# A whitening, window attention and mixture-of-experts kernel: the inverse root of its variances as one power operation on GpSimd

## The chip, the cores and the metric

The kernel runs on one core of one Trainium2 chip. The metric is the device time of one execution in microseconds, as the median of several executions.

## The reference

The input x is (16, 56, 56, 64) in float32, that is 50,176 tokens of 64 channels. Three stages follow one another.

```python
# 1. whitening (_iter_norm_whiten): groups of 16 channels, statistics over all tokens
cov = (1 - EPS) * cov + EPS * eye;  sigma = cov / trace
for _ in range(5): P = (3 * P - P @ P @ P @ sigma) / 2
x = gamma * (P / sqrt(trace)) @ (x - mu) + beta
# 2. attention in a window of 33 tokens, per image (3136 tokens)
kv = _ln_t(t)                                  # (v - mean) / sqrt(var + 1e-5), over 64 channels
out = softmax(scores * 64 ** -0.5) @ windows
out = (out - mean(out)) * rsqrt(var(out) + 1e-5) * gamma + beta
t = t + out
# 3. mixture of experts: 8 experts, top 2
n = _ln_t(t)
t = t + moe(n)    # n + sum over the two experts of weight * (gelu(n @ w1 + b1) @ w2 + b2)
```

So there are three layer norms per token: of the whitened tokens, of the attention's output and of the sum that goes into the experts.

## The kernel before, in words

All engines have instruction streams written out by hand, and semaphores alone order them against each other. There are three parts.

The first part (to about 78 us) loads x once, builds the Gram matrix on TensorE and column sums on VectorE, and computes the whitening matrix in a chain of small operations. GpSimd prepares constants in that time.

The middle part (about 78 to 535 us) does the whitening, the attention and the routing. The 16 images go in pairs (H = 2); a chunk is NB = 7 blocks of 64 tokens of both images of a pair (CH = 448 columns on 128 partitions), CPI = 7 chunks make a pair, and there are G = 56 chunks. The work is a software pipeline: in step g each engine does stage d of chunk g - d, so that a step holds one stage each of seven chunks. In the step function of each engine, `has(d)` says whether stage d has a chunk. The stages: 0 transposes and whitens a chunk, squares it for its variance and makes its norm xn; 1 transposes xn into keys; 2 computes the scores and their exponential; 3 does the product with the values, and scales the attention's output to t_s; 4 takes bn_stats of the residual sum and makes its norm tn; 5 transposes tn and spills it to HBM; 6 computes the router's logits. The routing (top 2 of 8) of finished pairs is cut into single VectorE operations, one per step (`route`).

The order inside a step, with the lines of the profile:

- TensorE: transposes of the x tiles of chunk g (L971, L964 out of `to_paired`), router logits of chunk g - 6 (L981, L984), whitening of chunk g (L979, L981, L984), product with the values of g - 3 (L1060), transposes of xn of g - 1 (L971, L964) and of tn of g - 5 (L971, L964), scores of g - 2 (L1082, L1087). L979 waits for L521's copy.
- ScalarE: copy of the transposed x (L521), copy of the logits (L526), square of the whitened chunk (L534) and its copy (L537), square of the attention's sums (L542), copy of the keys (L548), copy of the transposed tn (L558) and its store, exponential of the scores (L569), and last the logarithm (L574) and the exponential with scale -0.5 (L576) of the variances of the step, 7 per norm and up to 21 columns. L574 waits for the variances (semaphore s_w), L576 for L574.
- VectorE: sums of the squares (L790), the variances of stages 0 and 3 (L793, L795), bn_stats of stage 4, seven times (L800), and the variance out of them (L803 to L809), which raises s_w; one routing operation; then it waits for L576 and does a Newton step in three operations (L818, L820, L822) that corrects the approximate root; xn (L828), stored by the DMA queues as rows, from which the values come back with windows; seven scalings of the attention's output (L834); the scaled mean (L842), tn (L843) and a correction column (L845), which signals tn.
- GpSimd: beta added to the whitened chunk (L479, after xn), and the residual sum t_s + yb (L487), which waits for t_s of its chunk and for L845 of the step, and which bn_stats of the next step reads.
- SyncE issues the loads of x, the row stores after xn, and the loads of the values.

`sm` is the small tile for all of this: slot 4 has the variances (times C = 64), slots 6 and 7 the logarithm and the approximate root, 8 and 9 the Newton step and the result. `norms(has)` gives the range of the three norms that exist in the step.

The last part (about 535 us to the end) runs the experts, four pairs of them for each chunk, and is not touched.

Of the kernel before, what the change touches and what calls it, by code (L numbers as in the profile page):

```python
# [29 lines left out]
NB = 7  # L30
# [3 lines left out]
C = 64  # L34
# [9 lines left out]
EPS_LN = 1e-5  # L44
# [9 lines left out]
def hybrid_kernel(nc, x, g0, b0, g1, b1v, rw, w1, b1, w2, b2, k_eye, k_fold, k_group, k_block, k_band,  # L54
                  k_rank, k_sel, out):
    f32, bf16, f32r = mybir.dt.float32, mybir.dt.bfloat16, mybir.dt.float32r
    ALU, ACT, AX = mybir.AluOpType, mybir.ActivationFunctionType, mybir.AxisListType
# [8 lines left out]
    SCALE = float(C) ** -0.5  # L66
# [12 lines left out]
    with ctx:  # L79
        def sb(name, shape, dt=f32):  # L80
            return ctx.enter_context(nc.sbuf_tensor(name, shape, dt))
# [4 lines left out]
        def sem(name):  # L86
            return ctx.enter_context(nc.semaphore(name))
# [100 lines left out]
        sq = sb("sq", [128, 2, NB, C + 1])  # L188
# [5 lines left out]


        sm = sb("sm", [128, 10, 3, NB])
        top = sb("top", [128, 5, NB * CPI])

        tn_rows = t_s[:, 0:2, :, :].rearrange("p k b c -> p k (b c)")
# [15 lines left out]
        s_cd, s_cp, s_ca = sem("chain_dve"), sem("chain_pe"), sem("chain_act")  # L215
        s_x2 = [sem(f"x2_in{i}") for i in range(7)]
        s_xt, s_xts, s_y, s_ys, s_yb = sem("xt"), sem("xt_copied"), sem("y"), sem("y_copied"), sem("yb")
        s_v, s_w, s_ln, s_r, s_n = sem("norm_steps"), sem("norm_var"), sem("norm_log"), sem("norm_rsqrt"), sem("norm_newton")
        s_red, s_xn = sem("pv_squares_summed"), sem("xn")
        s_xnt, s_kts = sem("xn_t"), sem("keys_copied")  # L220
        s_pad, s_xw, s_vd = sem("pads_zeroed"), sem("xn_rows_stored"), [sem(f"values_in{i}") for i in range(2)]
# [1 line left out]
        s_sqy, s_sq, s_t = sem("y_squared"), sem("pv_squared"), sem("t_scaled")  # L223
# [13 lines left out]
        def wait(eng, s, n):  # L237

            if not isinstance(n, int) or n > 0:
                eng.wait_ge(s, n)  # L240
# [36 lines left out]
        def norms(has):  # L277

            lo = 0 if has(0) else 1 if has(3) else 2
            hi = 3 if has(4) else 2 if has(3) else 1  # L280
            return lo, hi
# [126 lines left out]
        def _(pool):  # L408
            v = nc.gpsimd
# [11 lines left out]
            v.memset(ones_h[:, :], 1.0)  # L421
            v.memset(white[:, :, :], 0.0)
            v.memset(ones, 1.0)
            v.memset(v_a[:, :, :, C], 1.0)
            zeros = sq[0:WIN].rearrange("p k b c -> p (k b c)")[:, 0:NP // 2 * H * C]
            v.memset(zeros, 0.0).then_inc(s_zero, 1)
# [45 lines left out]
            v.memset(keys_t[:, WIN + CPI * CH:], 0.0).then_inc(s_zero, 1)  # L472

            def step(g, c, has):
                if has(1):
                    q, cq = g - 1, prv(c, 1)
                    wait(pool, s_xn, g + 1 if has(0) else G)
                    ybc = yb[:, cq, :, 0:C]
                    v.tensor_tensor(ybc, ybc, bet1[:, :].unsqueeze(1).to_broadcast([128, NB, C]), ALU.add).then_inc(s_yb, 1)  # L479
                if has(3):  # L480
                    q, cq = g - 3, prv(c, 3)
                    sl = SLOT2[cq]
                    wait(pool, s_t, q + 1)
                    wait(pool, s_yb, q + 1)
                    if has(4):
                        wait(pool, s_tn, q)
                    v.tensor_tensor(resid[:, bass.ds(q * CH, CH)].rearrange("p (b c) -> p b c", b=NB), t_s[:, sl],  # L487
                                    yb[:, cq, :, 0:C], ALU.add).then_inc(s_t2, 1)
# [13 lines left out]
        def _(act):  # L502
            a = nc.scalar
# [13 lines left out]
            def step(g, c, has):  # L517
# [10 lines left out]
                if has(0):  # L528
                    wait(act, s_y, g + 1)
                    wait(act, s_w, g)  # L530
                    y_s = p01[:, 1, 0:NB * (C + 1)].rearrange("p (b c) -> p b c", b=NB)
                    if g == 0:
                        act.wait_ge(s_pad, 16 * 4)
                    a.activation(sq[:, 0], y_s, ACT.Square).then_inc(s_sqy, 1)  # L534
                    wait(act, s_t2, g - 6)
                    wait(act, s_tn, g - 6)
                    a.activation(yb[:, c], y_s, ACT.Copy).then_inc(s_ys, 1)  # L537
                if has(3):
                    q = g - 3
                    wait(act, s_o, q + 1)  # L540
                    wait(act, s_w, g)
                    a.activation(sq[:, 1], sums(q).rearrange("p (b c) -> p b c", b=NB),  # L542
                                 ACT.Square).then_inc(s_sq, 1)
                if has(1):
                    q, cq = g - 1, prv(c, 1)
                    wait(act, s_xnt, q + 1)
# [18 lines left out]
                if has(2):  # L565
# [1 line left out]
                    wait(act, s_s, q + 1)  # L567

                    a.activation(prob[:, :, :], p34[0:KEYS, :, 0:CH], ACT.Exp, scale=SCALE).then_inc(s_p, 1)  # L569
                lo, hi = norms(has)  # L570
                if lo < hi:

                    wait(act, s_w, g + 1)
                    a.activation(sm[:, 6, lo:hi, :], sm[:, 4, lo:hi, :], ACT.Ln, scale=1.0 / C).then_inc(s_ln, 1)  # L574
                    wait(act, s_ln, g + 1)
                    a.activation(sm[:, 7, lo:hi, :], sm[:, 6, lo:hi, :], ACT.Exp, scale=-0.5).then_inc(s_r, 1)  # L576

            for g in range(G):
                step(g, g % 7, lambda d, g=g: d <= g)
# [63 lines left out]
        def _(dve):  # L643
            v = nc.vector
# [16 lines left out]
            for k in range(2):  # L661
                last = v.tensor_reduce(colsum2[:, k, :], colsum.rearrange("p n c -> p c n"), AX.X, ALU.add)
# [116 lines left out]
            def step(g, c, has):  # L779
                lo, hi = norms(has)  # L780
# [9 lines left out]
                    v.tensor_reduce(sm[:, 0, of, :], sq[:, of, :, 0:C], AX.X, ALU.add).then_inc(s_red, 1)  # L790
                    wait(dve, s_red, g + 1)
                if has(0):
                    last = v.tensor_scalar(sm[:, 4, 0, :], sm[:, 0, 0, :], C * EPS_LN, None, ALU.add)  # L793
                if has(3):
                    last = v.scalar_tensor_tensor(sm[:, 4, 1, :], sq[:, 1, :, C], C * EPS_LN, sm[:, 0, 1, :], ALU.mult, ALU.add)  # L795
                if has(4):
                    wait(dve, s_t2, g - 3)
                    t4 = resid[:, bass.ds((g - 4) * CH, CH)].rearrange("p (b c) -> p b c", b=NB)
                    for b in range(NB):
                        last = v.bn_stats(st[:, b, :], t4[:, b, :])  # L800
                    last.then_inc(s_v, 1)
                    wait(dve, s_v, (g - 4) * 3 + 1)
                    v.tensor_tensor(sm[:, 0, 2, :], st[:, :, 1], st[:, :, 4], ALU.add)  # L803
                    v.tensor_tensor(sm[:, 1, 2, :], st[:, :, 1], st[:, :, 4], ALU.subtract)
                    v.scalar_tensor_tensor(sm[:, 2, 2, :], st[:, :, 2], C * EPS_LN, st[:, :, 5], ALU.add, ALU.add).then_inc(s_v, 1)
                    wait(dve, s_v, (g - 4) * 3 + 2)
                    v.tensor_tensor(sm[:, 4, 2, :], sm[:, 1, 2, :], sm[:, 1, 2, :], ALU.mult).then_inc(s_v, 1)
                    wait(dve, s_v, (g - 4) * 3 + 3)
                    last = v.scalar_tensor_tensor(sm[:, 4, 2, :], sm[:, 4, 2, :], C / 4.0, sm[:, 2, 2, :], ALU.mult, ALU.add)  # L809
                if lo < hi:  # L810
                    last.then_inc(s_w, 1)
                im, k = route_at(g, 0)
# [2 lines left out]
                if lo < hi:  # L815

                    wait(dve, s_r, g + 1)
                    v.tensor_tensor(sm[:, 8, lo:hi, :], sm[:, 4, lo:hi, :], sm[:, 7, lo:hi, :], ALU.mult).then_inc(s_n, 1)  # L818
                    wait(dve, s_n, g * 3 + 1)
                    v.scalar_tensor_tensor(sm[:, 8, lo:hi, :], sm[:, 8, lo:hi, :], -0.5 / C, sm[:, 7, lo:hi, :], ALU.mult, ALU.mult).then_inc(s_n, 1)  # L820
                    wait(dve, s_n, g * 3 + 2)
                    v.scalar_tensor_tensor(sm[:, 9, lo:hi, :], sm[:, 8, lo:hi, :], 1.5, sm[:, 7, lo:hi, :], ALU.add, ALU.mult).then_inc(s_n, 1)  # L822
                    wait(dve, s_n, g * 3 + 3)
                if has(0):
                    wait(dve, s_xnt, g)
                    wait(dve, s_xw, 48 * g)
# [404 lines left out]
```

## Time and profile before

| | us |
|---|---|
| median of 3 executions | 1111.7 |
| lowest and highest | 1108.69, 1125.13 |
| the profiled execution's own time | 1112.64 |
| its span in the profile | 1110.9 |
| TensorE busy | 1048.4 |
| VectorE busy | 904.3 |
| ScalarE busy | 565.4 |
| GpSimd busy | 148.3 |

The profile has one execution. PE is TensorE (PEld its weight loads), DVE is VectorE, ACT is ScalarE, POOL is GpSimd; L12 is line 12 of the kernel. A row of the timeline reads: start in us, duration in us, engine, line, operation, output<-input, shapes, count, and in brackets how long the engine stood idle before it and what ended that. In groups by line, the columns are busy us and mean ns of one, then the idle time before them. PEclk is TensorE's granted clock in tenths of full speed, in 40 equal slices; 1.00 in a table of windows is 2.4 GHz and 0.50 is 1.2 GHz. The chain that ended last is followed back from the last instruction through what released each one.

### The profile page before, as it was taken

Reading aid. Unit: us, or ns where it says so; the run is one execution under the profiler, and the core shown is the slowest. Engines: PE = TensorE matmul, PEld = TensorE weight load, DVE = VectorE, ACT = ScalarE, POOL = GpSimd, SP = SyncE. Lnnn points to the kernel's source line nnn. Section 1 sums busy time; section 2 is a strip of 40 time slices with the busy share of each in tenths; the row PEclk is TensorE's granted clock in tenths of the full one; section 3 lists DMA queues with packets and bytes.
Section 4 is the critical chain, followed back from the end, with each engine's and each line's share of the span. In section 5 each row is a group of like instructions: output and inputs, shape, how many; then the busy total and the mean of one; then the engine's idle time right before and its main releaser. Section 6 shows DMA issues by size and latency. Waiting matters only on the chain.

```text
span 1110.9 us, 26094 instructions
## 1 busy us (share of the span) xinstructions
PE 1048.4 (94%) x9158; PEld 692.8 (62%) x9158; DVE 904.3 (81%) x2575; ACT 565.4 (51%) x917; POOL 148.3 (13%) x179
## 2 busy tenths in 40 slices
PE   7947999999999999998799999999999999999998
PEld 7935777777777777776455555555555555555553
DVE  6944888887888887887788888888888888888785
ACT  0014655655566555653455555555555555555553
POOL 7021232232223222231000000000000000000000
PEclk9959999998999999995799999999999999999999
DMA  9604555554555555543122222222222222222221
GB/s 290 238 9 105 142 131 147 136 133 113 143 138 136 142 135 137 136 120 90 42 67 70 71 66 67 71 70 66 74 66 67 68 73 66 70 71 66 67 71 44
DMA packets 244750, 111.51 MB, mean 100 GB/s; under 512 B 199392, under 2 KB 242656, under 8 KB 243888
## 3 DMA queue, kind: packets, MB, share of 16 engines
q1 hardware_dynamic: 235456, 96.91, 35.1%
q10 hardware_dynamic: 8064, 12.85, 3.4%
q8 instruction: 51, 0.84, 0.3%
q0 software_dynamic: 1136, 0.56, 0.2%
q14 instruction: 43, 0.35, 0.1%
HBM read 71.60 MB, written 38.67 MB: 99 GB/s over the span
## 4 chain that ended last, share of the span: by engine, by line
PE 82%; ACT 9%; DVE 4%; issue 3%; DMA 2%; SPq 0%; POOL 0%; DVEq 0%; ACTq 0%; POOLq 0%
PE p L1138 17%; PE p L1113 16%; PE p L1123 10%; PE p L1087 7%; PE p L971 7%; ACT prob L569 5%; PE p L1060 4%; PE p L964 4%; PE p L981 4%; ACT xt_s L521 3%; PE p L1082 3%; DMA resid<-in_x_dram 2%; PE p L1134 2%; PE p L979 2%; PE p L1008 2%
## 5 line engine op out<-in xcount | busy, mean ns | idle before, releaser
L586 ACT ACTIVATE arena<-p,b_s 128x896 f32<-128x896 f32 x224 | 225.5, 1007 | 231.0 <-PE p L1113 229.6
L890 DVE TENSOR_TENSOR arena<-arena,p 128x896 f32<-128x896 f32 x224 | 242.5, 1083 | 76.4 <-PE p L1123 74.8
L1138 PE MATMUL p<-arena,w_s 128*64 128x448 f32 x896 | 215.2, 559 | 0.3 <-DVE arena L890 0.3
L1113 PE MATMUL p<-thl,w_hi 128*128 128x448 f32 x448 | 165.2, 450 | 0.4 <-DVE thl L862 0.4
L1113 PE MATMUL p<-thl,w_lo 128*128 128x448 f32 x448 | 127.3, 365 | 0.0
L1123 PE MATMUL p<-arena,selector 128*128 128x448 bf16 x448 | 123.9, 358 | 1.8 <-DVE arena L890 1.4
L1123 PEld LDWEIGHTS p<-arena,selector 128*128 128x128 bf16 x448 | 25.4, 97 | 159.0 <-issue 116.9
L1113 PEld LDWEIGHTS p<-thl,w_hi 128*128 128x128 f32 x448 | 85.6, 192 | 21.2 <-issue 0.6
L479 POOL TENSOR_TENSOR yb<-yb,bet 128x448 f32<-128x448 f32 x56 | 59.2, 1058 | 253.5 <-DVE xn_s L828 253.5
L569 ACT ACTIVATE prob<-p 96x896 f32<-96x896 f32 x56 | 51.1, 912 | 78.2 <-PE p L1087 78.2
L1113 PEld LDWEIGHTS p<-thl,w_lo 128*128 128x128 f32 x448 | 84.9, 189 | 7.6
L1087 PEld LDWEIGHTS p<-arena 64*96 64x96 f32 x1568 | 74.2, 167 | 20.3 <-issue 20.3
L790 DVE TENSOR_REDUCE sm<-sq 128x14 f32<-128x896 f32 (+1 forms) x59 | 61.2, 1038 | 29.4 <-ACT sq L542 22.6
L1087 PE MATMUL p<-arena 64*96 64x64 f32 x1568 | 82.0, 255 | 0.0
L834 DVE SCALAR_TENSOR_TENSOR t_s<-p,sm,gam 128x64 f32<-128x64 f32 x392 | 80.0, 276 | 0.1
L1138 PEld LDWEIGHTS p<-arena,w_s 128*64 128x64 f32 x896 | 49.5, 135 | 44.0 <-issue 34.0
L534 ACT ACTIVATE sq<-p 128x455 f32<-128x455 f32 x56 | 30.8, 550 | 89.6 <-PE p L984 89.6
L487 POOL TENSOR_TENSOR resid<-t_s,yb 128x448 f32 (+1 forms) x56 | 59.2, 1057 | 81.3 <-DVE comb L845 80.9
L862 DVE TENSOR_TENSOR thl<-arena,thl 64x896 fp32r<-64x896 f32 x56 | 60.7, 1085 | 2.6 <-ACT thl L599 0.9
L971 PE MATMUL p<-eye,arena 128*128 128x128 f32 x336 | 59.4, 286 | 0.7 <-DVE arena L927 0.7
L800 DVE BATCH_NORM_STATS2 st<-resid 128x6 f32<-128x64 f32 x392 | 54.8, 211 | 1.3 <-POOL resid L487 1.3
L599 ACT ACTIVATE thl<-arena 64x896 fp32r<-64x896 f32 x56 | 53.0, 946 | 4.7 <-DMA arena<-tn_spill 3.2
(177 smaller groups left out, 1640.6 us busy)
## 6 DMA issues: line engine op xcount, KB each, us to landing
tn_spill<-tnt_s ACTq DMA_DIRECT2D x56, 224.0 KB, 2.7
arena<-tn_spill SPq DMA_DIRECT2D x56, 224.0 KB, 3.4
t_s<-tn_spill SPq DMA_DIRECT2D x56, 224.0 KB, 2.5
arena<-in_x_dram SPq DMA_DIRECT2D x112, 96.0 KB, 2.6
xn_rows<-xn_s SPq DMA_DIRECT2D x56, 192.0 KB, 2.1
out_dram<-arena SPq DMA_DIRECT2D x112, 96.0 KB, 1.8
resid<-in_x_dram SPq DMA_DIRECT2D x6, 1568.0 KB, 14.2
v_a<-xn_rows SPq DMA_DIRECT2D x56, 168.0 KB, 3.3
```

Of the source, the lines that this page charges most:

```text
L479: v.tensor_tensor(ybc, ybc, bet1[:, :].unsqueeze(1).to_broadcast([128, NB, C]), ALU.add).then_inc(s_yb, 1)
L569: a.activation(prob[:, :, :], p34[0:KEYS, :, 0:CH], ACT.Exp, scale=SCALE).then_inc(s_p, 1)
L586: a.activation(hid[:, j % 2, :].rearrange("p (h n) -> p h n", h=H), (p34 if j % 2 == 0 else p56)[:, :, 0:CH], ACT.Gelu, bias=b1_s[:, j:j + ...
L790: v.tensor_reduce(sm[:, 0, of, :], sq[:, of, :, 0:C], AX.X, ALU.add).then_inc(s_red, 1)
L834: last = v.scalar_tensor_tensor(t_s[:, sl3, b, :], o_s[:, b, 0:C], sm[:, 9, 1, b:b + 1], gam1[:, :], ALU.mult, ALU.mult)
L862: v.tensor_tensor(thl[64:128, c], tn_in[:, c].rearrange("p (h n) -> p h n", h=H), thl[0:64, c].bitcast(f32), ALU.subtract).then_inc(s_lo, 1)
L890: v.tensor_tensor(gated[:, j % 2, :].rearrange("p (h n) -> p h n", h=H), hid[:, j % 2, :].rearrange("p (h n) -> p h n", h=H), p01[:, :, 0: ...
L971: t.transpose(dst[:, b * 128:(b + 1) * 128], src[:, b * 128:(b + 1) * 128], eye[:, :])
L1087: last = t.matmul(p34[0:KEYS, h, b * BLK:(b + 1) * BLK], keys_t[r, at_b:at_b + KEYS], keys_t[r, at_b + WIN:at_b + WIN + BLK], start=False, ...
L1113: last = t.matmul(bank[:, h, 0:CH], w[:, 128 * j:128 * (j + 1)], thl[:, c, h, :], start=(k == 0), stop=(k == 1))
L1123: last = t.matmul(p01[:, h, 0:CH], selector[:, (4 * h + j) * 128:(4 * h + j + 1) * 128], ct_s[:, c, :], start=True, stop=True)
L1138: last = t.matmul(p2[64 * h:64 * h + 64, 0:CH], w2_s[:, j, :], gated[:, j % 2, h * CH:(h + 1) * CH], start=False, stop=(j == 3))
```

## The change

The variances are now divided by C before the root: Square on ScalarE gets the scale 1/8 (SCALE, whose square is 1/64), and the constants of L793, L807 and L809 follow. GpSimd raises the variances to the power -0.5, with a tile of -0.5 as the second operand, at the head of its step, and gives s_r; the logarithm, the exponential and the three operations of the Newton step are gone. The first part keeps its own logarithm and exponential.

```diff
+        halves = sb("halves", [128, 3, NB])
...
+            v.memset(halves[:, :, :], -0.5)
...
             def step(g, c, has):
+                lo, hi = norms(has)
+                if lo < hi:
+                    wait(pool, s_w, g + 1)
+                    v.tensor_tensor(sm[:, 9, lo:hi, :], sm[:, 4, lo:hi, :], halves[:, lo:hi, :], ALU.pow).then_inc(s_r, 1)
                 if has(1):
...
-                    a.activation(sq[:, 0], y_s, ACT.Square).then_inc(s_sqy, 1)
+                    a.activation(sq[:, 0], y_s, ACT.Square, scale=SCALE).then_inc(s_sqy, 1)
...
-                                 ACT.Square).then_inc(s_sq, 1)
+                                 ACT.Square, scale=SCALE).then_inc(s_sq, 1)
...
-                lo, hi = norms(has)
-                if lo < hi:
-                    wait(act, s_w, g + 1)
-                    a.activation(sm[:, 6, lo:hi, :], sm[:, 4, lo:hi, :], ACT.Ln, scale=1.0 / C).then_inc(s_ln, 1)
-                    wait(act, s_ln, g + 1)
-                    a.activation(sm[:, 7, lo:hi, :], sm[:, 6, lo:hi, :], ACT.Exp, scale=-0.5).then_inc(s_r, 1)
...
-                    last = v.tensor_scalar(sm[:, 4, 0, :], sm[:, 0, 0, :], C * EPS_LN, None, ALU.add)
+                    last = v.tensor_scalar(sm[:, 4, 0, :], sm[:, 0, 0, :], EPS_LN, None, ALU.add)
...
-                    v.tensor_tensor(sm[:, 4, 2, :], sm[:, 1, 2, :], sm[:, 1, 2, :], ALU.mult).then_inc(s_v, 1)
+                    v.scalar_tensor_tensor(sm[:, 4, 2, :], sm[:, 1, 2, :], 0.25, sm[:, 1, 2, :], ALU.mult, ALU.mult).then_inc(s_v, 1)
...
-                    last = v.scalar_tensor_tensor(sm[:, 4, 2, :], sm[:, 4, 2, :], C / 4.0, sm[:, 2, 2, :], ALU.mult, ALU.add)
+                    last = v.scalar_tensor_tensor(sm[:, 4, 2, :], sm[:, 2, 2, :], 1.0 / C, sm[:, 4, 2, :], ALU.mult, ALU.add)
...
                     wait(dve, s_r, g + 1)
-                    v.tensor_tensor(sm[:, 8, lo:hi, :], sm[:, 4, lo:hi, :], sm[:, 7, lo:hi, :], ALU.mult).then_inc(s_n, 1)
-                    wait(dve, s_n, g * 3 + 1)
-                    v.scalar_tensor_tensor(sm[:, 8, lo:hi, :], sm[:, 8, lo:hi, :], -0.5 / C, sm[:, 7, lo:hi, :], ALU.mult, ALU.mult).then_inc(s_n, 1)
-                    wait(dve, s_n, g * 3 + 2)
-                    v.scalar_tensor_tensor(sm[:, 9, lo:hi, :], sm[:, 8, lo:hi, :], 1.5, sm[:, 7, lo:hi, :], ALU.add, ALU.mult).then_inc(s_n, 1)
-                    wait(dve, s_n, g * 3 + 3)
```

## Rows read from the trace of the kernel before

**Rows 1.** The page: busy time of each engine, TensorE's clock in 40 slices, the chain that ended last
```profile
PE 1048.4 (94%) x9158; PEld 692.8 (62%) x9158; DVE 904.3 (81%) x2575; ACT 565.4 (51%) x917; POOL 148.3 (13%) x179
...
PEclk9959999998999999995799999999999999999999
...
PE 82%; ACT 9%; DVE 4%; issue 3%; DMA 2%; SPq 0%; POOL 0%; DVEq 0%; ACTq 0%; POOLq 0%
```

**Rows 2.** Timeline of 212.5 to 222.5 us, rows of ScalarE and TensorE (columns as below)
```profile
213.05 0.91 ACT L569 ACTIVATE prob<-p 96x896 f32<-96x896 f32 x1 [1.30 <-PE p L1087]
...
213.86 0.21 ACT L574 ACTIVATE sm<-sm 128x21 f32<-128x21 f32 x1
214.10 0.22 ACT L576 ACTIVATE sm<-sm 128x21 f32<-128x21 f32 x1
214.22 0.62 ACT L521 ACTIVATE xt_s<-p,neg_mean 128x448 f32<-128x448 f32 x1
...
214.44 0.29 PE L984 MATMUL p<-router,tnt_s 128*64 128x8 f32 x4
...
214.99 0.35 PE L979 MATMUL p<-bet_rows,ones_h 128*128 128x455 bf16 x1 [0.25 <-ACT xt_s L521]
...
222.41 0.35 PE L979 MATMUL p<-bet_rows,ones_h 128*128 128x455 bf16 x1 [0.25 <-ACT xt_s L521]
```

**Rows 3.** Who waited for whom in 100 to 500 us (total us, times, longest us)
```profile
PE p L979 <- ACT xt_s L521: 14.9, 51, 1.2
```

**Rows 4.** The same timeline, rows of VectorE and GpSimd, and the transposes of tn
```profile
215.00 0.63 DVE L828 TENSOR_TENSOR xn_s<-yb,sm 128x448 f32<-128x448 f32 x1
...
215.71 1.04 POOL L479 TENSOR_TENSOR yb<-yb,bet 128x448 f32<-128x448 f32 x1 [4.15 <-DVE xn_s L828]
...
217.50 0.17 DVE L845 TENSOR_TENSOR comb<-yb,sm 128x7 f32<-128x7 f32 x1
...
217.76 0.55 PE L971 MATMUL p<-eye,tn_s 128*128 128x128 f32 x3
217.85 1.09 DVE L790 TENSOR_REDUCE sm<-sq 128x14 f32<-128x896 f32 x1 [0.19 <-ACT sq L542]
...
217.94 1.06 POOL L487 TENSOR_TENSOR resid<-t_s,yb 128x448 f32 x1 [1.19 <-DVE comb L845]
...
219.13 0.98 DVE L800 BATCH_NORM_STATS2 st<-resid 128x6 f32<-128x64 f32 x7
...
220.71 0.17 DVE L809 SCALAR_TENSOR_TENSOR sm<-sm 128x7 f32<-128x7 f32 x1
220.79 0.56 DVE L752 SCALAR_TENSOR_TENSOR arena<-arena 128x392 f32<-128x392 f32 x1
...
222.42 0.63 DVE L828 TENSOR_TENSOR xn_s<-yb,sm 128x448 f32<-128x448 f32 x1
```

**Rows 5.** Groups by line, shapes apart, of the whole span
```profile
L754 DVE TENSOR_TENSOR top<-top 128x49 f32<-128x49 f32 x8 | 1.6, 203 | 0.0
...
L454 POOL TENSOR_TENSOR arena<-arena 128x193 f32<-128x193 f32 x2 | 1.1, 543 | 0.2
...
L759 DVE RECIPROCAL top<-top 128x49 f32<-128x49 f32 x2 | 0.9, 456 | 0.0
```

**Rows 6.** Timeline of 505 to 530 us, the drain of the middle part
```profile
513.83 0.90 PE L971 MATMUL p<-eye,tn_s 128*128 128x128 f32 x3 [0.92 <-DVE comb L845]
...
523.11 0.90 PE L971 MATMUL p<-eye,tn_s 128*128 128x128 f32 x3 [1.30 <-DVE comb L845]
```

**Rows 7.** Timeline of 245 to 258 us, a step in which the clock fell
```profile
245.08 0.35 PE L979 MATMUL p<-bet_rows,ones_h 128*128 128x455 bf16 x1 [0.25 <-ACT xt_s L521]
...
247.07 1.78 PE L1060 MATMUL p<-v_a,prob 96*64 96x65 f32 x28 [0.70 <-issue]
...
257.58 0.56 PE L979 MATMUL p<-bet_rows,ones_h 128*128 128x455 bf16 x1
```

**Rows 8.** Busy time of 100 to 110 us (PE, PEld, DVE, ACT, POOL, then granted clock)
```profile
100.00:110.00 10.00, 6.88 (x98) 5.35 (x95) 6.51 (x30) 5.49 (x12) 2.09 (x2) 1.00 0.57 123
```

More of the change, by code:

```diff
@@ L217, in hybrid_kernel @@
         s_xt, s_xts, s_y, s_ys, s_yb = sem("xt"), sem("xt_copied"), sem("y"), sem("y_copied"), sem("yb")
-        s_v, s_w, s_ln, s_r, s_n = sem("norm_steps"), sem("norm_var"), sem("norm_log"), sem("norm_rsqrt"), sem("norm_newton")
+        s_v, s_w, s_r = sem("norm_steps"), sem("norm_var"), sem("norm_rsqrt")
         s_red, s_xn = sem("pv_squares_summed"), sem("xn")
```

## The prediction

> **What bounds the kernel now.** I began with the page: TensorE is busy 94% of the span, holds 82% of the chain that ended last, and its clock is at full speed in most slices [rows 1]. The change touches only the middle part (about 78 to 535 us, 56 steps of one chunk each), so I went to the timeline of one undisturbed step. From one L979 to the next it lasts 222.41 - 214.99 = 7.42 us [rows 2]. Read downwards, those rows show a closed ring: the scores end, ScalarE takes the exponential (L569), then L574 and L576, which the change removes, and only then the copy L521, on which TensorE's L979 waits. TensorE had finished the router products at 214.44 + 0.29 = 214.73 and stood idle for 0.25 us. The table of waits says that this is the rule: 51 such waits with 14.9 us in 100 to 500 us, of which only the first ones are long (up to 1.2 us) [rows 3]. So a step is TensorE's own work, 7.42 - 0.25 = 7.17 us, and 0.25 us of waiting for ScalarE.
>
> Beside it runs a second ring, over VectorE and GpSimd, nearly as long [rows 4]. Start with L828 (xn) at 215.00. The last VectorE instruction of the step, L845, ends at 217.67, 2.67 us later. The residual sum on GpSimd (L487) starts 0.27 us later, takes 1.06 us and ends at 219.00; bn_stats (L800) of the next step reads its result, I allow 0.10 us between them (at most 0.13 is to be seen), and from the start of L800 to the end of L809, which gives the variances free, go 220.88 - 219.13 = 1.75 us. From there to the next L828 at 222.42 it is 1.54 us. The sum is 2.67 + 0.27 + 1.06 + 0.10 + 1.75 + 1.54 = 7.39 us: this ring has 0.03 us of slack against 7.42. Whoever speeds up the first ring meets the second at once.
>
> **The change part by part.** Call P the time from the end of L809 to the start of L828. Before, P = 1.54 us: ScalarE is held by L569, does two small activations, and then VectorE does three steps (L818, L820, L822). All five go. In their place P = delay to GpSimd + power + delay back. From the end of L828 (215.63) to L479 on GpSimd (215.71) I read 0.08 us [rows 4]; back I allow 0.10 us. GpSimd is idle then: L487 has ended at 219.00, the variances come at 220.88, and the next L479 waits for xn. The routing operation, which stands between L809 and the wait on VectorE, still runs beside it (L752 here, 0.56 us [rows 4], hidden by any longer P).
>
> *ScalarE's side.* L521 would follow L569 as L574 does now: 213.86 instead of 214.22, 0.36 us earlier. L979 follows 0.77 us after the start of L521, so at 214.63, while TensorE is free at 214.73. The step loses the whole 0.25 us and becomes TensorE's 7.17 us. In the 49 steps with the short wait that is 49 x 0.25 = 12.3 us. In five early ones, where TensorE waits longer, 5 x 0.36 = 1.8 us.
>
> *What the second ring allows.* The step is max(7.17, 5.85 + P), with 5.85 = 7.39 - 1.54. The full gain needs P up to 1.32 us; P = 1.57 gives the old 7.42; 2% more (22 us over 50 steps, 0.44 each, so 7.86) needs P = 2.01. The other consumer, the transposes of tn (L971), starts at 217.76, 0.09 us after L845 ends [rows 4]; its slack becomes 0.09 + (1.54 - P) - 0.25, used up at P = 1.38, so it asks for the same.
>
> *The power itself* is in no row. Lower end: as an addition. On GpSimd 193 elements take 0.543 us [rows 5] and 448 take 1.06 [rows 4], so 2.03 ns an element and 0.15 us fixed; 21 elements would take 0.19 us. For a harder function the nearest row is VectorE's reciprocal: 456 ns for 49 elements against 203 ns for a two-input operation of that size [rows 5]. That is 5.2 ns more on top of about 1.07 ns an element ((630 - 203) / (448 - 49), from L828), 5.8 times as much. If a power is a logarithm, a product and an exponential in software, and each counts as a reciprocal on GpSimd, it is 3 x 5.8 x 2.03 x 21 = 0.74 us, and 0.89 us with the fixed part. I take this value. For the upper end I take ten such functions instead of three, 2.63 us; nothing in the rows excludes it, or more. With 0.89, P = 0.08 + 0.89 + 0.10 = 1.07 us, under 1.32.
>
> In terms of the power alone the three marks are therefore 1.14 us (full gain), 1.39 us (no gain) and 1.83 us (2% slower).
>
> *The drain.* After the last chunks the transposes of tn wait for VectorE (0.92 and 1.30 us, [rows 6]), because ScalarE's L574 stands behind an exponential that waits for TensorE. The power does not stand there; these 2.2 us go, and I count 2.0.
>
> *Costed at nothing.* The memset of the constants is one small instruction at the start, under the loads. The scale in Square and the constants in L793, L807 and L809 change no instruction count. L542's output feeds L790 as before.
>
> *Sum* against the profiled execution's own 1112.64 us: 1112.64 - 12.3 - 1.8 - 2.0 = 1096.5. That execution is 0.9 us above the median of the three (1111.7), so 1095.6 by the median; I say 1096.
>
> A rule that speaks against it: on GpSimd, L479 and L487 take 1.04 and 1.06 us [rows 4], beside VectorE work that has one operand in PSUM or is a one-input reduction, so no row shows a GpSimd operation beside a two-input SBUF operation. The Trainium skill (GPSIMD Engine Reference, section "Key points") says that GpSimd shares its SBUF interfaces with VectorE and contends with instructions that have two SBUF inputs; several routing operations are just that.
>
> **The rivals.**
> 1. *The power is slow and the second ring takes over* (the other side of zero). Place: VectorE waits ahead of L828; behind it are queued xn, the seven scalings of the attention output, tn, and on GpSimd L479 and L487, which wait for them. It decides from a power of 1.39 us. With 2.0 us P = 2.18, the step 8.03 us, 50 x 0.61 = 30 us more: 1142; with the upper end of 2.63 us 50 x 1.24 = 62 more, 1174. For it: the ring has only 0.03 us of slack now, and the power's price is a guess. Against it: 21 elements are few.
> 2. *Part of the gain.* A power between 1.14 and 1.39 us gives 1096 to 1112; 1105 for the middle.
> 3. *Contention.* The power stands still while the routing operation reads SBUF: 0.56 us more, P = 1.63, step 7.48, 50 x 0.06 = 3 us above the old steps, with the drain about 1114.
> 4. *The clock falls with the new wait.* One step had TensorE waiting 0.70 us before L1060, and its products then ran slow: that step lasted 257.58 - 245.08 = 12.50 us, 5.08 more [rows 7]. If a slow power causes such a wait (from about P = 2) in every other step, 25 x 5.08 = 127 us more, about 1240. Against it: from 100 to 110 us TensorE is busy 6.88 of 10 us with the granted clock at 1.00 [rows 8].
> 5. *More than the sum.* The wait in rows 7 stands ahead of the product with the values, and I take it for their transfer. If xn comes 0.47 us sooner (1.54 - 1.07) the values do too, and that stretch is gone: 5.08 less, 1091; faster by over 2% needs 1089.
> 6. *The removed work is not on the path*: then it stays at 1112. The 0.25 us behind L521 in nearly every step speaks against that, so I fold it into rival 2.
>
> **How the numbers follow.** Forecast (about 1090 to 1101) 0.48; rival 2 0.10; rival 3 0.04; rival 5 beyond 2% 0.05; rival 1 with a loss under 2% 0.09, over 2% 0.20; rival 4 0.04. So faster by over 2% 0.05, within 2% 0.48 + 0.10 + 0.04 + 0.09 = 0.71, slower by over 2% 0.20 + 0.04 = 0.24; 2% is about what a measurement of this kernel tells from no change. The range starts at 1088 (0.03 below it) and goes to 1150 (a power of about 2.1 us; some 0.16 above it). The likeliest case's own range is 1090 to 1101.
>
> **What would show it.** In the profile after: no wait of L979 for L521, steps of 7.17 us, L521 0.36 us sooner after L569, a power row on GpSimd near 0.9 us, L828 about 1.07 us after L809, TensorE busier than 94%. Wrong is the estimate if the power's row is above 1.14 us; wrong is the arithmetic of the second ring if the step is not 5.85 + P then, or if VectorE still waits ahead of L828 for something other than the power. If L979 still waits with L521 early, another producer was hidden behind it.

## The result: 17% slower, and the profile after

The changed kernel takes 1308.74 us in the median of four runs (1306.98 to 1311.81), the kernel before 1112.42 us beside it; the ratio is 1.173 with a 95% interval of 1.166 to 1.180. The forecast was 1096 us in a range of 1088 to 1150. Here and below, some executions of a kernel fall into a slower state and are left out of its ratio. The profiled execution took 1306.98 us, with a span of 1305.2 us.

The page of the changed kernel, the same three lines as in [rows 1]:

```profile
PE 1216.1 (93%) x9158; PEld 824.6 (63%) x9158; DVE 873.1 (67%) x2395; ACT 554.3 (42%) x797; POOL 363.7 (28%) x240
...
PEclk9957666666666666666666699999999999999999
...
PE 79%; DVE 10%; POOL 6%; issue 2%; DMA 2%; ACT 1%; SPq 0%; POOLq 0%; DVEq 0%; ACTq 0%
```

TensorE is busy for 1216 us instead of 1048, with the same 9158 matmuls: it has no more to do, but its clock stands at 0.6 in the whole middle part, which now fills 19 slices. GpSimd has come into the chain that ended last with 6%, and VectorE's share has gone from 4% to 10%.

The groups by line and shape show why. The power's line (columns: busy us and mean ns of one, idle time before it):

```profile
L480 POOL TENSOR_TENSOR sm<-sm,halves 128x21 f32<-128x21 f32 x52 | 198.1, 3810 | 184.2 <-DVE sm L808 184.2
...
L480 POOL TENSOR_TENSOR sm<-sm,halves 128x14 f32<-128x14 f32 x4 | 10.9, 2725 | 13.8 <-DVE sm L794 8.2 <-DVE sm L808 5.6
...
L480 POOL TENSOR_TENSOR sm<-sm,halves 128x7 f32<-128x7 f32 x4 | 6.2, 1561 | 9.3 <-DVE sm L792 8.6 <-DVE sm L808 0.7
```

A power on 21 elements takes 3.81 us in the mean, on 14 elements 2.73 and on 7 elements 1.56. Each of these means mixes two durations (3.70 and 3.96 us for 21 elements), of which the longer comes from contention with VectorE, taken up below. The shorter ones are 3.70, 2.60 and 1.49 us; that is (3.70 - 1.49) / 14 = 158 ns an element and about 0.39 us fixed. An addition costs 2.03 ns an element [rows 4, 5]; the power costs 78 times that. The prediction had 0.89 us, and 2.63 us as the upper end.

A step in the timeline of the changed kernel, rows that answer to [rows 2] and [rows 4] (L575 is the exponential of the scores that was L569; L527 the copy L521; L972 was L979; L808 was L809; L821 was L828; L964 was L971; L838, L493 and L799 were L845, L487 and L800):

```profile
247.59 0.91 ACT L575 ACTIVATE prob<-p 96x896 f32<-96x896 f32 x1 [1.30 <-PE p L1080]
247.77 0.17 DVE L808 SCALAR_TENSOR_TENSOR sm<-sm 128x7 f32<-128x7 f32 x1
247.85 0.56 DVE L745 TENSOR_TENSOR arena<-arena,rank 128x392 f32<-128x392 f32 x1
...
248.02 3.96 POOL L480 TENSOR_TENSOR sm<-sm,halves 128x21 f32<-128x21 f32 x1 [4.50 <-DVE sm L808]
...
248.40 0.62 ACT L527 ACTIVATE xt_s<-p,neg_mean 128x448 f32<-128x448 f32 x1
...
248.99 0.29 PE L977 MATMUL p<-router,tnt_s 128*64 128x8 f32 x4
...
249.21 0.37 PE L972 MATMUL p<-bet_rows,ones_h 128*128 128x455 bf16 x1
...
252.01 0.63 DVE L821 TENSOR_TENSOR xn_s<-yb,sm 128x448 f32<-128x448 f32 x1 [3.60 <-POOL sm L480]
...
252.69 0.55 PE L964 MATMUL p<-eye,xn_s 128*128 128x128 f32 x3 [1.36 <-DVE xn_s L821]
...
254.51 0.16 DVE L838 TENSOR_TENSOR comb<-yb,sm 128x7 f32<-128x7 f32 x1
...
254.72 0.90 PE L964 MATMUL p<-eye,tn_s 128*128 128x128 f32 x3 [1.22 <-DVE comb L838]
254.94 1.06 POOL L493 TENSOR_TENSOR resid<-t_s,yb 128x448 f32 x1 [1.16 <-DVE comb L838]
...
256.03 0.99 DVE L799 BATCH_NORM_STATS2 st<-resid 128x6 f32<-128x64 f32 x7
...
257.63 0.17 DVE L808 SCALAR_TENSOR_TENSOR sm<-sm 128x7 f32<-128x7 f32 x1
257.71 0.55 DVE L747 TENSOR_REDUCE top<-arena 128x49 f32<-128x392 f32 x1
257.87 3.70 POOL L480 TENSOR_TENSOR sm<-sm,halves 128x21 f32<-128x21 f32 x1 [1.87 <-DVE sm L808]
...
261.61 0.63 DVE L821 TENSOR_TENSOR xn_s<-yb,sm 128x448 f32<-128x448 f32 x1 [3.34 <-POOL sm L480]
```

Read from above: ScalarE's part is as predicted. The copy L527 starts 0.81 us after the exponential (1.17 before), and L972 follows the router products (248.99 + 0.29) without the old wait of 0.25 us. But VectorE's L808 gives the variances at 247.94, and L821 starts at 252.01: P is 4.07 us, where it was 1.54 before. TensorE waits twice, 1.36 us for xn and 1.22 us for tn. The second ring then closes as the prediction had it: L821 to the end of L838 2.66 us, 0.27 us to L493, 1.06 us for it, 0.03 us to L799, and 1.77 us from there to the end of L808 (257.80). That is 5.79 us (the prediction had 5.85, with 0.10 us allowed where 0.03 are seen). From one L821 to the next it is 9.60 us.

The last of the transposes shows the second effect: three products of tn take 0.90 us, against 0.55 us for the same three of xn just ahead. The clock has gone to the lower of its two levels between them. Over 120 to 480 us the granted clock was 0.64 (columns: PE, PEld, DVE, ACT and POOL busy, clock, DMA share, GB/s):

```profile
120.00:480.00 360.00, 335.40 (x3148) 267.31 (x3147) 185.73 (x847) 136.46 (x253) 187.77 (x95) 0.64 0.39 93
...
244.04:254.28 10.24, 8.10 (x111) 6.28 (x109) 5.63 (x26) 5.27 (x10) 5.02 (x2) 1.00 0.41 99
254.28:278.17 23.89, 23.45 (x189) 18.83 (x191) 12.53 (x56) 7.71 (x14) 12.93 (x7) 0.50 0.38 89
```

The last two rows are one turn of a pattern that repeats through the whole stretch, three steps to a turn. In the stretch at the full clock TensorE makes both waits, and the clock falls in the second one (254.28, with L964 at 254.72). At the lower level its own work is the longer part of a step and it hardly waits (23.45 of 23.89 us busy). When the clock comes back the waits do too. The table of waits (120 to 480 us) has each of them ten times, once a turn:

```profile
PE p L964 <- DVE xn_s L821: 12.4, 10, 1.4
PE p L964 <- DVE comb L838: 12.2, 10, 1.2
```

Steps of 9.5 to 9.8 us are therefore only about one in three. The other two of a turn, which run wholly or partly at the lower level, take 11.8 to 12.6 us, and the mean over the 54 starts of L821 is (695.55 - 93.29) / 53 = 11.36 us, against (501.82 - 94.47) / 53 = 7.69 us before. 53 x 3.67 = 195 us is the whole loss.

### The profile page after: what moved, and what is told of

It reads as the page before. It is cut to its first block, busy times and chain, and to the rows that moved or that the text cites. A ratio compares the mean times of both kernels' runs of the same rounds, so it can differ in the third digit from the quotient of the medians.

```text
span 1305.2 us, 25855 instructions
## 1 busy us (share of the span) xinstructions
PE 1216.1 (93%) x9158; PEld 824.6 (63%) x9158; DVE 873.1 (67%) x2395; ACT 554.3 (42%) x797; POOL 363.7 (28%) x240
## 4 chain that ended last, share of the span: by engine, by line
PE 79%; DVE 10%; POOL 6%; issue 2%; DMA 2%; ACT 1%; SPq 0%; POOLq 0%; DVEq 0%; ACTq 0%
PE p L1131 15%; PE p L1106 14%; PE p L1116 8%; PE p L974 8%; PE p L964 7%; PE p L1080 7%; POOL sm L480 6%; PE p L957 4%; PE p L1053 4%; PE p L1075 3%; PE p L977 2%; DVE t_s L827 2%; DMA resid<-in_x_dram 2%; PE p L1127 2%; DVE sm L789 2%
## 5 line engine op out<-in xcount | busy, mean ns | idle before, releaser
L480 POOL TENSOR_TENSOR sm<-sm,halves 128x21 f32<-128x21 f32 (+2 forms) x60 | 215.3, 3588 | 207.3 <-DVE sm L808 190.5
L821 DVE TENSOR_TENSOR xn_s<-yb,sm 128x448 f32<-128x448 f32 x56 | 35.0, 626 | 193.4 <-POOL sm L480 193.4
L1080 PEld LDWEIGHTS p<-arena 64*96 64x96 f32 x1568 | 109.9, 236 | 31.6 <-issue 31.6
L1080 PE MATMUL p<-arena 64*96 64x64 f32 x1568 | 119.5, 327 | 0.0
L575 ACT ACTIVATE prob<-p 96x896 f32<-96x896 f32 x56 | 51.2, 914 | 129.3 <-PE p L1080 129.3
L493 POOL TENSOR_TENSOR resid<-t_s,yb 128x448 f32 (+1 forms) x56 | 59.1, 1056 | 67.6 <-DVE comb L838 67.2
L974 PEld LDWEIGHTS p<-white,xt_s 128*128 128x128 f32 x336 | 72.5, 287 | 1.7
L974 PE MATMUL p<-white,xt_s 128*128 128x130 f32 x336 | 72.3, 376 | 0.0
L964 PE MATMUL p<-eye,arena 128*128 128x128 f32 x336 | 71.4, 331 | 0.7 <-DVE arena L920 0.7
```

The source lines that it names most:

```text
L480: v.tensor_tensor(sm[:, 9, lo:hi, :], sm[:, 4, lo:hi, :], halves[:, lo:hi, :], ALU.pow).then_inc(s_r, 1)
L964: t.transpose(dst[:, b * 128:(b + 1) * 128], src[:, b * 128:(b + 1) * 128], eye[:, :])
L974: t.matmul(dst[:, b * 2 * width:(b + 1) * 2 * width], src[:, b * 128:(b + 1) * 128], weights, start=alone, stop=alone)
L1080: last = t.matmul(p34[0:KEYS, h, b * BLK:(b + 1) * BLK], keys_t[r, at_b:at_b + KEYS], keys_t[r, at_b + WIN:at_b + WIN + BLK], start=False, ...
```

## The experiments

Twelve kernels ran, each beside the kernel before, which took 1116.2, 1118.1 and 1115.4 us in the three groups (1107 to 1142). Where a kernel computes something else, the text says what.

### Is the price of the power all that was wrong?

**e1_mult** puts a product of two constants in the power's place, so the norms are not normalised but scaled by 0.25.

```diff
-  v.tensor_tensor(sm[:, 9, lo:hi, :], sm[:, 4, lo:hi, :], halves[:, lo:hi, :], ALU.pow).then_inc(s_r, 1)
+  v.tensor_tensor(sm[:, 9, lo:hi, :], halves[:, lo:hi, :], halves[:, lo:hi, :], ALU.mult).then_inc(s_r, 1)
```

> The power is replaced by a product of two constants of the same shape (so the norms are scaled by 0.25 instead of their inverse root); every wait stays. Theory A (the price of the power is all that was wrong, and the two rings are as in the prediction): the product takes about 0.2 us, P is about 0.4 us, TensorE no longer waits for the copy of the transposed x, the step is 7.17 us and the time about 1096 us (1090 to 1101). Rival B (the move itself costs: another producer was hidden behind the copy, or GpSimd in the ring is slow to answer): the step stays at 7.42 us or more and the time at 1110 us or more.

Measured: 1102.72 us (1090 to 1133), ratio 0.985 (0.974 to 0.996). The forecast of 1096 us was a ratio of 0.985 too. The wait for the copy is gone from the table of waits. But the median step is 7.39 us, not 7.17. The first row below is from the kernel before, the second is the same wait in e1_mult (120 to 480 us), ahead of the product with the values:

```profile
PE p L1060 <- issue: 3.2, 10, 0.7
...
PE p L1053 <- issue: 11.2, 23, 1.1
```

So theory A holds in size, with a longer wait for the values that I had not named. The interval reaches 0.996, so the time alone hardly excludes rival B (1110 us or more); what speaks against it is that the wait for the copy is gone. The values are taken up below.

**d14, d21, d30, d38** measure the second ring dose by dose. Ahead of the constant product GpSimd multiplies a spare tile with itself: 480 elements, 830, twice 590 and twice 800. They too have no normalisation.

```diff
+  wait(pool, s_spare, g + 1)
+  v.tensor_tensor(spare[:, :], spare[:, :], spare[:, :], ALU.mult).then_inc(s_spare, 1)
   v.tensor_tensor(sm[:, 9, lo:hi, :], halves[:, lo:hi, :], halves[:, lo:hi, :], ALU.mult).then_inc(s_r, 1)
```

> As e1_mult, with one product on 480 elements of a spare tile ahead of it on GpSimd, after the wait for the variances: together about 1.4 us. Theory A: P is about 1.55 us, the step 5.85 + 1.55 = 7.40 us, the time 1108 to 1112 us, as before the change. Rival B (TensorE or ScalarE bind at another place): a step that does not follow 5.85 + P.

> As d14 with 830 elements: together about 2.1 us, P about 2.25 us. Theory A without a fall of the clock: step 8.10 us, time 1109 + 50 x 0.68 - 2 = about 1142 us, granted clock 1.00 from 120 to 480 us. Theory C (a wait of TensorE of about 0.9 us in each step is enough for the clock to fall): windows with a clock of 0.5 to 0.8 in the middle part and a time over 1180 us.

> As d38 with products on 590 elements: together about 2.8 us, P about 3.0 us, between d21 (P = 2.11, clock 1.00, step 7.78) and d38. The ring alone: step 8.6 to 8.8 us and 1165 to 1180 us with the clock at 1.00. Theory C with a threshold between: TensorE now waits about 1.5 us in a step, in two pieces; if that is enough for the clock to fall, the mean clock in 120 to 480 us is 0.7 to 0.9 and the time over 1200 us.

> No power: two products on 800 elements of a spare tile and the constant product on GpSimd, together about 3.8 us, as long as the power on 21 elements. Theory A (the power matters by its duration alone, with the clock's fall following from it): the same as the changed kernel, 1290 to 1320 us, with two slow steps in three. Rival F (the power has an effect of its own, for example on VectorE or on the SBUF interfaces): clearly below the changed kernel, about 1220 us.

| kernel | P, us | steps of the ring's length, us | clock, 120 to 480 us | time, us | ratio |
|---|---|---|---|---|---|
| d14 | 1.28 or 1.53 | 7.32 (median) | 1.00 | 1104.4 | 0.989 (0.982 to 0.996) |
| d21 | 1.86 or 2.11 | 7.65 or 7.90 | 1.00 | 1120.8 | 1.007 (1.002 to 1.011) |
| d30 | 2.80 or 2.96 | 8.57 or 8.75 | 0.70 | 1248.7 | 1.118 (1.107 to 1.128) |
| d38 | 3.50 or 3.66 | 9.29 or 9.45 | 0.67 | 1298.3 | 1.167 (1.160 to 1.173) |
| changed kernel | 3.82 or 4.07 | 9.60 or 9.85 | 0.64 | 1308.7 | 1.173 |

From d30 on the third column has the shortest steps, one in two or three; the clock falls in them, and the others are longer. These steps are P + 5.79 us within 0.05 us from d21 on (7.90 - 2.11, 8.57 - 2.80, 9.60 - 3.81). d14 lies at the edge: its P leaves a ring of 7.07 or 7.32 us, TensorE is as long, and the time of 1104 us is a little under the 1108 to 1112 expected. d21's time was over-estimated (1142 expected, 1121 measured) for two reasons. P came out at 1.86 or 2.11 us and not at 2.25, and the kernel before does not run at 7.42 us in the mean but at 7.69. d38 met its forecast (1290 to 1320): ordinary products nearly as long as the power give 1298 us, so the power acts by its duration.

Between d21 and d30 lies the jump. 0.9 us more in a step should make 50 us; it made 128. (d30's profiled execution took 1261.75 us, 13 over its median, so its rows overstate the loss somewhat.) The windows and waits of the two, d21 first:

```profile
120.00:480.00 360.00, 339.54 (x4656) 271.01 (x4656) 276.90 (x1245) 197.49 (x376) 185.12 (x187) 1.00 0.55 136
```

```profile
PE p L968 <- DVE comb L842: 16.4, 37, 0.7
```

```profile
120.00:480.00 360.00, 341.78 (x3455) 275.23 (x3454) 203.83 (x923) 149.08 (x278) 161.16 (x172) 0.70 0.41 100
```

```profile
PE p L970 <- DVE comb L844: 16.8, 14, 1.2
```

In d21 TensorE waits for tn 0.44 us at a time (0.7 at most) and its clock is 1.00 throughout. In d30 the same wait is 1.2 us in the shortest steps (14 of them in 35 steps). The clock falls there, and one to three longer steps follow, of 10.9 to 12.7 us.

### Is the rest the clock?

**e3_fill** and **e3b_fill** are the changed kernel, with its power, and 18 or 10 small products on TensorE ahead of each of its two waits, into columns of a PSUM bank that nobody reads.

```diff
+  for _ in range(18):        # 10 in e3b_fill
+      t.matmul(p56[0:64, 1, 448:512], eye[:, 0:64], eye[:, 0:64], start=True, stop=True)
   wait(pe, s_xn, q + 1)
```

> The changed kernel with its power, and 18 small products each (into unused columns of a PSUM bank) on TensorE ahead of its waits for xn and for tn, about 1.2 us each at the full clock, where it waits 1.36 and 1.22 us. Theory C (the fall of the clock adds to the second ring): the clock stays up, the step is 5.85 + 4.07 = 9.92 us and the time about 1109 + 50 x 2.5 = 1235 us, lower than the changed kernel although TensorE has more to do. Rival D (the clock does not matter, the ring through GpSimd sets all of the step): no gain, 1309 us. Rival E (the filler does not hold the clock, and the slow steps become longer by 36 slow products, over 3 us each): over 1380 us.

> As e3_fill with 10 products ahead of each wait instead of 18 (36 of them had cost TensorE 11.30 - 7.17 = 4.1 us a step, 0.11 us each, and made it the bound with the clock at 1.00). 20 make 2.3 us, so TensorE has 9.45 us a step. Theory C (part of the loss is the clock, which falls when TensorE waits long enough in a step): clock 1.00, step about 9.7 us as in the full-clock steps of the changed kernel, time about 1222 us against 1309. Rival D (the ring with the power alone makes the mean step of 11.4 us): 1300 us or more.

e3_fill measured 1302.46 us, where 1235 had been expected: the clock stood at 1.00, but TensorE was busy for all 360 of the 360 us; a step was 11.30 us because the filler itself was the bound (4.1 us of it, where I had reckoned 2.4). It told nothing of the ring. e3b_fill measured 1218.89 us (1218.3 to 1220.0), where 1222 had been expected:

```profile
120.00:480.00 360.00, 355.29 (x5219) 301.54 (x5219) 222.14 (x1003) 156.84 (x299) 219.44 (x112) 1.00 0.44 109
```

The mean step is (609.78 - 89.42) / 54 = 9.64 us, which is the ring (3.82 or 4.07 and 5.79 us). TensorE has more to do than in the changed kernel and the kernel is 1308.7 - 1218.9 = 90 us faster. The loss of 196 us thus divides into about 106 us of ring (53 x (9.64 - 7.69) = 103) and about 90 us of clock. The two kernels were not timed side by side; their ratios to the kernel before, 1.173 and 1.094, give 88 us.

### What stands behind the copy?

**g_sp** and **e1_sp** change the order of SyncE's queue, in the kernel before and in e1_mult.

```diff
-                if g + 3 < G:
-                    tokens_in2(g + 3)
                 if g < G:
                     rows_out(g)
+                if g + 3 < G:
+                    tokens_in2(g + 3)
```

> The kernel before, with one change in SyncE's queue: rows_out(g) is issued ahead of the loads of x for chunk g + 3. Theory G (a third ring: loads of x 2.3 us, row stores 1.8, their landing 2 to 3, loads of the values 1.0, one after another, about 7.4 us or more with jitter, makes TensorE wait ahead of the product with the values): the loads of x hide the landing, these waits (3.2 us in 120 to 480 us, and the fall of the clock after one of them) go, mean step 7.45 instead of 7.69 us, 8 to 13 us less than before. Rival: the landing only moves, no difference.

> e1_mult (constant product instead of the power) with the same reordering. In e1_mult the wait for the copy (11.6 us in 120 to 480 us) was gone, but the waits ahead of the product with the values had grown from 3.2 to 11.2 us. Theory G: these go too, the step is 7.17 to 7.2 us, 1.5 to 2% below e1_mult, about 2.8% below before. Rival: they come from the transfer's own jitter and stay.

Both expectations failed: g_sp took 1157.45 us (ratio 1.030, 1.022 to 1.038) and e1_sp 1103.23 us (ratio 0.989), as e1_mult, with waits for the values of 10.8 us where e1_mult had 11.2. Queue and product with the values in g_sp (SPq: time in which the queue's issues went out):

```profile
301.62 0.38 SPq L345 DMA_DIRECT2D xn_rows<-xn_s  x1
...
302.88 1.04 PE L1060 MATMUL p<-v_a,prob 96*64 96x65 f32 x28 [0.64 <-issue]
...
303.24 3.25 SPq L339 DMA_DIRECT2D arena<-in_x_dram  x4
...
306.59 1.16 SPq L356 DMA_DIRECT2D arena<-xn_rows  x2
```

The four loads of x occupy the queue for 3.25 us after the row stores, so the loads of the values go out at 306.59 us, 4.97 us after the first row store, and TensorE waits 0.64 us for values. In the kernel before, only the landing lies between, and it is 278.96 - 274.50 = 4.46 us:

```profile
274.50 0.59 SPq L345 DMA_DIRECT2D xn_rows<-xn_s  x1
...
278.96 0.91 SPq L356 DMA_DIRECT2D v_a<-xn_rows  x2
```

This turn of the kernel before is one of its longer ones. In the mean over 120 to 480 us the loads of the values go out 3.5 us after the first row store in the kernel before and 4.4 us in g_sp, so 1 us later. The waits for them are 15.0 us in 120 to 480 us where they were 3.2; the profiled execution of g_sp was the longest of six (1174 us), so 15.0 is more than is typical. The old order put the loads of x into the time in which SyncE waits for the next xn. In e1_mult that time is mostly gone:

```profile
274.05 0.90 SPq L357 DMA_DIRECT2D v_a<-xn_rows  x2
...
274.85 0.63 DVE L821 TENSOR_TENSOR xn_s<-yb,sm 128x448 f32<-128x448 f32 x1 [0.24 <-POOL sm L480]
...
274.99 2.23 SPq L340 DMA_DIRECT2D arena<-in_x_dram  x4
...
277.27 0.59 SPq L346 DMA_DIRECT2D xn_rows<-xn_s  x1
...
277.90 1.14 SPq L349 DMA_DIRECT2D xn_rows<-xn_s  x2
...
277.94 1.04 PE L1053 MATMUL p<-v_a,prob 96*64 96x65 f32 x28 [0.84 <-issue]
...
282.26 0.90 SPq L357 DMA_DIRECT2D arena<-xn_rows  x2
```

xn is ready at 275.48, but the loads of x hold the queue to 277.22, and the rows go out then; after their landing the values follow at 282.26. Values 0.90, loads of x 2.23, rows 1.77 and the rest landing make 8.2 us for this turn. In 37 of the 48 turns of 120 to 480 us the rows go out right behind the loads of x (within 0.1 us); in the kernel before it is 14 of 47.

**e1_halfx** takes two of the four loads of x out of e1_mult; the last block of each chunk is then a constant.

```diff
-                for tile, tokens in pieces(x_tokens, g, x2[:, SLOT3[g % 7], :]):
-                    sp.dma_start(tile, tokens).then_inc(s_x2[g % 7], 16)
+                for k, (tile, tokens) in enumerate(pieces(x_tokens, g, x2[:, SLOT3[g % 7], :])):
+                    if k % 2 == 0:
+                        sp.dma_start(tile, tokens).then_inc(s_x2[g % 7], 16)
```

> e1_mult with only two of the four loads of x in each step (the last block of a chunk is not loaded; part of the tile keeps a constant). Theory H (SyncE's queue of issues is the next bound behind the copy: values 0.9, loads of x 2.3, row stores 1.8, landing 2 to 3, one after another): the queue has 1.1 us more air, the waits ahead of the product with the values (11.2 us in 120 to 480) fall under 4 us, the median step to 7.2 us and the time to about 1085 us. Rival (the waits are the transfer's own jitter): as e1_mult, 1098 to 1103 us.

Measured: 1086.31 us (1081 to 1088), ratio 0.972 (0.964 to 0.980); median step 7.19 us, and the wait:

```profile
PE p L1055 <- issue: 2.6, 8, 0.6
```

All three numbers are as theory H had them, and in no turn do the rows stand right behind the loads of x. So once the copy does not bind, what binds is SyncE's side, at a mean step of 7.61 us against TensorE's 7.17. Whether it is the queue or the transfers is not separated: half the loads also means half the bytes, and the time from the first row store to the loads of the values fell too, from 3.9 to 3.3 us in the mean.

### Other ways to the same end

**f_nonewton** leaves the Newton step out of the kernel before; **f_moved** also puts ScalarE's pair behind the next step's copy.

```diff
-  a.activation(sm[:, 7, lo:hi, :], sm[:, 6, lo:hi, :], ACT.Exp, scale=-0.5).then_inc(s_r, 1)
+  a.activation(sm[:, 9, lo:hi, :], sm[:, 6, lo:hi, :], ACT.Exp, scale=-0.5).then_inc(s_r, 1)
...
-  v.tensor_tensor(sm[:, 8, lo:hi, :], sm[:, 4, lo:hi, :], sm[:, 7, lo:hi, :], ALU.mult).then_inc(s_n, 1)
...
```

> The kernel before without the Newton step alone (three VectorE operations, 0.65 us a step). By the prediction's first ring nothing is won, since TensorE waits for ScalarE's copy and not for VectorE: step 7.42 us, ratio 0.995 to 1.005. Rival (VectorE is the bound): 0.97 or less.

> The kernel before, without the Newton step, and with logarithm and exponential on ScalarE behind the copy L521 of the next step instead of ahead of it (the norms are then as exact as the two table functions). TensorE's wait for the copy (11.6 us in 120 to 480) goes as in e1_mult; P stays about 1.5 us (later by 0.6, shorter by the Newton step's 0.65). By the rings: as d14 (P = 1.55), ratio to before 0.985 to 0.99, about 1100 us. Rival: ScalarE's delay of L526 and L534 by 0.45 us makes TensorE or VectorE wait elsewhere, and nothing is won.

f_nonewton measured 1107.47 us, ratio 0.992 (0.988 to 0.996). The median step is 7.42 us as expected, with the wait for the copy untouched, but the ratio lies just under the 0.995 to 1.005 forecast. The small gain is consistent with the shorter waits for the values, 1.7 us where the kernel before had 3.2, and with a clock of 1.00 over 120 to 480 us where it had 0.98. That this comes from the shorter VectorE work is not shown:

```profile
PE p L973 <- ACT xt_s L521: 12.2, 48, 0.3
...
PE p L1054 <- issue: 1.7, 3, 0.9
```

f_moved gave 1101 to 1132 us in four runs, too widely spread to tell. Its shortest steps are 7.24 us, so the first ring did open; in its profile, taken of the longest of the four, TensorE waited 8.2 us for the values, and a stretch of three steps at the low clock came after one such wait. That the copy can be freed this way is shown, that it pays is not.

## Why the prediction was wrong

*The bound.* Right, as far as it went. Two rings, ScalarE's copy with 0.25 us of wait and VectorE's with GpSimd's almost as long, were the picture; e1_mult removed the first wait entirely, and the dose series gave the second ring's constant as 5.79 us against 5.85. A third, SyncE's queue, was missing.

*The power itself.* This is the step that failed first: 0.89 us predicted, 3.81 measured, above the upper end of 2.63. It put P at 1.07 us, under the 1.32 us that the second ring allows, where 3.82 or 4.07 us were measured; so the forecast gain became 106 us of loss by the ring. The prediction said that nothing in the rows excluded more, and then cut the range at 2.1 us as if the upper end were one. Scaling VectorE's reciprocal by 5.8 and by three has no bearing on how GpSimd computes a power: 158 ns an element instead of 35 was measured. The second step that failed is the clock: its fall stood in the sum at nothing, and it cost 90 us more.

*Rival 1* (the slow power, the second ring takes over) is what happened, with a chance of 0.29 in the prediction. Put with the measured power into its formula, the step is 5.85 + 0.18 + 3.81 = 9.84 us and the time 1112.6 + 50 x 2.42 = 1234 us; the ring alone measured 1219 (e3b_fill).

*Rival 4* (the clock falls) happened as well, and was priced as an alternative at 1240 us where it had to be added. It was to come from about P = 2 on; it was absent at 2.11 and present at 2.8. Its chance of 0.04 was too small, for [rows 8] was read too strongly: TensorE idle for a third of the time at full clock for 10 us did not show that the clock stays up for 50 steps.

*Rival 3* (contention): right in kind, smaller in size (0.56 us forecast, 0.25 measured), and only beside some routing operations. [rows 4] had no GpSimd operation beside a VectorE operation with two SBUF inputs. d21 has them (its L773 is a routing product of two SBUF tensors):

```profile
304.62 0.17 DVE L812 SCALAR_TENSOR_TENSOR sm<-sm 128x7 f32<-128x7 f32 x1
304.70 0.56 DVE L773 TENSOR_TENSOR arena<-arena,top 128x392 f32<-128x392 f32 x1
304.87 1.82 POOL L483 TENSOR_TENSOR spare<-spare 128x830 f32<-128x830 f32 x1 [1.87 <-DVE sm L812]
...
306.65 0.21 POOL L484 TENSOR_TENSOR sm<-halves 128x21 f32<-128x21 f32 x1
306.90 0.63 DVE L825 TENSOR_TENSOR xn_s<-yb,sm 128x448 f32<-128x448 f32 x1 [1.64 <-POOL sm L484]
```

Here the product on 830 elements takes 1.82 us. In the steps whose routing operation is a reduction, a copy or a reciprocal, or that have none, the same one takes 1.57 us, as here:

```profile
258.75 1.57 POOL L483 TENSOR_TENSOR spare<-spare 128x830 f32<-128x830 f32 x1 [1.87 <-DVE sm L812]
```

In the same way 480 elements take 1.24 and 0.99 us, the constant product of 21 elements in e1_mult 0.47 and 0.22 us, and the power 3.96 and 3.70 us, as the two steps in the timeline above show (beside L745 and beside L747). In 120 to 500 us of each trace every one of these operations has one of its two durations, by this rule. In all of them GpSimd starts 0.17 us after VectorE and runs 0.39 us beside it. In d30 and d38 it starts 0.1 us later, the overlap is 0.30 us, and the cost is 0.16 us (1.68 and 1.52 us):

```profile
243.98 0.56 DVE L751 TENSOR_TENSOR arena<-arena,rank 128x392 f32<-128x392 f32 x1
244.23 1.68 POOL L483 TENSOR_TENSOR spare<-spare 128x800 f32<-128x800 f32 x1 [1.97 <-DVE sm L814]
```

So the cost goes with the overlap, of which there are only these two values, and not with which of these operations GpSimd does. The Trainium skill (GPSIMD Engine Reference, section "Key points"), cited in the prediction, says that GpSimd contends with VectorE instructions that have two SBUF inputs. These traces agree with it. The 0.25 us is also why the steps come in two lengths.

*ScalarE's side and the sum.* 12.3 + 1.8 + 2.0 us of gain were forecast for a cheap operation. e1_mult gave 1.5% (16 us), but not by these terms alone: the wait for the copy went, and the waits for the values rose from 3.2 to 11.2 us in 360 us. Rival 5 expected the opposite, that an earlier xn would bring the values earlier. SyncE's side, with the loads of x ahead of the rows, was the hidden producer; the prediction never added up that queue. That e1_mult's 1.5% equals the forecast's is in part luck. The profiled executions have spans of 1110.9 and 1098.7 us; of these 12.2 us, 3.6 lie ahead of the third xn (94.47 and 90.83), only 4.1 in the 53 steps behind it (7.69 and 7.61 us in the mean), where 12.3 were forecast, and 4.4 behind the last xn, where 2.0 were.

## What to carry to other kernels

Before a function moves to another engine, look for a row of that function on that engine; if there is none, measure one instance first, since the price an element may be far above an addition's (78 times here), and do not close the range with a guess. When a loop has several rings of nearly equal length, write down each one's length, with the queues of the transfers as rings of their own: removing the wait of one shows the next, here mean steps of 7.69 us before, 7.61 with the copy freed and 7.33 with half the loads of x gone from the queue, over TensorE's own 7.17. If a new wait falls on TensorE, price the clock on top of the wait and not instead of it.

## What the runs showed of the hardware

- A power on GpSimd (TENSOR_TENSOR, float32, 128 partitions) takes 1.49, 2.60 and 3.70 us for 7, 14 and 21 elements when nothing contends with it (changed kernel): 158 ns an element.
- A GpSimd operation that overlaps a VectorE operation with two SBUF inputs takes longer: by 0.25 us for an overlap of 0.39 us (1.57 to 1.82, 0.99 to 1.24, 3.70 to 3.96) and by 0.16 us for one of 0.30 us (1.52 to 1.68). Beside the one-input routing operations it does not.
- With waits of about 0.44 us for tn (d21) TensorE kept 2.4 GHz in 120 to 480 us; with waits of up to 1.2 us (d30) and of 1.1 to 1.4 and 1.2 us (changed kernel) it ran 60 and 72% of that time at 1.2 GHz (mean clock 0.70 and 0.64). Small products in the waiting time kept it at 2.4 GHz and were worth 90 us of 1309. What exactly in the waits lets the clock fall stays open. The length of one wait alone does not decide it: in the kernel before it fell (at 246.95 us) in a wait of 0.70 us [rows 7], and in d14 it stayed at 1.00 over one of 1.33 us (at 369.93 us).
